# Attention maxima as two 64-row products side by side, in place of two 128-row products on block-diagonal keys

## The reference, cut to what matters

```python
scores = jnp.einsum('bhqd,bhkd->bhqk', query, key) / jnp.sqrt(D_K)
scores = jnp.where(m == 0, NEG_INF, scores)        # second layer only
probs = jax.nn.softmax(scores, axis=-1)
out = jnp.einsum('bhqk,bhkd->bhqd', probs, value)
...
x = x + jnp.tanh(g_xattn[1]) * (out @ Wo + bo)
```

## Time and profile before

| | |
|---|---|
| median of 3 runs | 2743.58 us (2742.97 to 2744.24) |
| the profiled execution | 2744.99 us |
| its span, first to last instruction | 2743.2 us |
| PE busy | 90% of the span, 12840 products |
| DVE, ACT, POOL busy | 53%, 39%, 18% |
| mean granted TensorE clock | 0.955 of full |
| attention, layer 0 / layer 1, one iteration in steady state | 52.82 us / 65.83 us |

### The profile page before, as it was taken

The page is one execution under the profiler, slowest core; times in us unless marked ns, Lnnn a source line. Parts: engine busy times, 40 slices in busy tenths (PEclk is TensorE's granted clock), DMA queues, the critical chain, the costliest instruction groups (busy, mean ns, idle before and its releaser), DMA issues. The chain is left out here.

```text
span 2743.2 us, 32089 instructions
## 1 busy us (share of the span) xinstructions
PE 2480.5 (90%) x12840; PEld 1860.6 (68%) x12864; DVE 1463.2 (53%) x2222; ACT 1078.3 (39%) x1734; POOL 505.4 (18%) x411
## 2 busy tenths in 40 slices
PE   4899999779999999996489999999579999999997
PEld 3557667458888888885355566665467788778776
DVE  4455565232222222211655665553488888888887
ACT  3233443243222222222223333332355666666564
POOL 1011211252000000001101111111462222222221
PEclk8799999889999999998699999999799999999999
DMA  3002111232001100102210111111321010101100
GB/s 129 31 16 81 59 47 47 86 114 81 16 31 46 46 27 20 47 31 75 95 41 28 59 59 59 59 44 62 100 82 53 16 46 32 47 16 34 44 16 31
DMA packets 87941, 140.92 MB, mean 51 GB/s; under 512 B 4848, under 2 KB 27760, under 8 KB 87792
## 3 DMA queue, kind: packets, MB, share of 16 engines
q1 hardware_dynamic: 87792, 138.87, 14.9%
HBM read 105.30 MB, written 33.55 MB: 51 GB/s over the span
## 5 line engine op out<-in xcount | busy, mean ns | idle before, releaser
L56 PE MATMUL l_ffn_hid<-l_ffn_xT_hi,l_ffn_w_hi 128*128 128x512 f32 x1024 | 406.0, 397 | 29.3 <-POOL l_ffn_w_lo L1124 29.3
L56 PE MATMUL l_ffn_acc<-l_ffn_w_hi,l_ffn_h_hi 128*128 128x512 f32 x1024 | 402.6, 393 | 18.1 <-DVE l_ffn_h_lo L1299 18.1
L56 PE MATMUL l_ffn_hid<-l_ffn_xT_hi,l_ffn_w_lo 128*128 128x512 f32 x1024 | 402.0, 393 | 0.0
L56 PE MATMUL l_ffn_hid<-l_ffn_xT_lo,l_ffn_w_hi 128*128 128x512 f32 x1024 | 401.9, 392 | 0.0
L56 PE MATMUL l_ffn_acc<-l_ffn_w_lo,l_ffn_h_hi 128*128 128x512 f32 x1024 | 399.5, 390 | 0.0
L56 PE MATMUL l_ffn_acc<-l_ffn_w_hi,l_ffn_h_lo 128*128 128x512 f32 x1024 | 399.2, 390 | 0.0
L1269 DVE TENSOR_TENSOR l_ffn_h_lo<-l_ffn_full,l_ffn_h_hi 128x512 fp32r<-128x512 f32 x128 | 88.6, 692 | 501.0 <-ACT l_ffn_h_hi L1181 501.0
L1136 POOL TENSOR_TENSOR l_ffn_at_next<-l_ffn_at_next,l_ffn_at_grid 128x512 f32<-128x512 f32 x128 | 187.5, 1465 | 491.7 <-ACT l_ffn_at_next L1197 491.6
L1176 ACT ACTIVATE l_ffn_full<-l_ffn_hid,l_ffn_b 128x512 f32<-128x512 f32 x128 | 88.2, 689 | 447.8 <-PE l_ffn_hid L56 447.8
L56 PEld LDWEIGHTS l_ffn_hid<-l_ffn_xT_hi,l_ffn_w_hi 128*128 128x128 f32 x1024 | 194.5, 190 | 76.0 <-POOL l_ffn_w_lo L1124 36.4
L56 PEld LDWEIGHTS l_ffn_acc<-l_ffn_w_hi,l_ffn_h_hi 128*128 128x128 f32 x1024 | 192.7, 188 | 65.0 <-DVE l_ffn_h_lo L1299 25.9
(11 more groups left out here) (191 smaller groups left out, 4309.3 us busy)
## 6 DMA issues: line engine op xcount, KB each, us to landing
stream<-l_att_xg SPq DMA_DIRECT2D x16, 1024.0 KB, 4.3
l_ffn_x_in<-stream SPq DMA_DIRECT2D x16, 1024.0 KB, 5.5
l_ffn_stage<-in_l_w SPq DMA_DIRECT2D x64, 256.0 KB, 2.8
l_ffn_xg<-stream SPq DMA_DIRECT2D x16, 1024.0 KB, 5.5
l_att_x_in<-in_x SPq DMA_DIRECT2D x8, 1024.0 KB, 6.5
l_att_xg<-in_x SPq DMA_DIRECT2D x8, 1024.0 KB, 5.3
stream<-l_ffn_xg SPq DMA_DIRECT2D x8, 1024.0 KB, 4.3
l_att_x_in<-stream SPq DMA_DIRECT2D x8, 1024.0 KB, 6.7
```

Source lines behind the costliest of these rows:

```text
L56: done = nc.tensor.matmul(out, lhs[a], rhs[b], start=first and n == 0, stop=last and n == len(passes) - 1)
```

## The change

In PE's `max_of` the product of half a takes only the 64 partitions on which its two heads lie, both of the weights and of the keys: partitions 0 to 63 for heads 0 and 1, 64 to 127 for heads 2 and 3. The zero rows of `keys.bd` outside a half are no longer multiplied; the result is the same. The two products are issued next to each other, on different rows of the array and to different banks. With the mask, both identity products come first, then both halves (before: identity, half, identity, half). Each half increments `max_ps`, so that DVE's waits count two per step. Number and size of the reductions, the weight loads (one ahead of each product) and the order around `max_of` stay.

```diff
@@ mask_front (DVE)
-                    dve.wait_ge(max_ps, NM * it)
+                    dve.wait_ge(max_ps, 2 * NM * it)
@@ max_of (DVE)
-                dve.wait_ge(max_ps, NM * it + m + 1)
+                dve.wait_ge(max_ps, 2 * (NM * it + m + 1))
@@ max_of (PE)
+                to = [score[:, 2 * (m % 2) + a, 0:2 * KEYS].rearrange("p (h k) -> p h k", h=2)
+                      for a in range(2)]
+                if masked:
+                    for a in range(2):
+                        nc.tensor.matmul(to[a], ident_bf[:, :], mask_add[:, q, :].unsqueeze(1)
+                                         .broadcast_to([P, 2, KEYS]), start=True, stop=False)
                 for a in range(2):
-                    to = score[:, 2 * (m % 2) + a, 0:2 * KEYS].rearrange("p (h k) -> p h k", h=2)
-                    if masked:
-                        nc.tensor.matmul(to, ident_bf[:, :], mask_add[:, q, :].unsqueeze(1)
-                                         .broadcast_to([P, 2, KEYS]), start=True, stop=False)
-                    done = nc.tensor.matmul(to, qT[it % QB][0][:, t, q * P:(q + 1) * P],
-                                            keys.bd[:, b, t, 2 * a:2 * a + 2, :],
-                                            start=not masked, stop=True)
-                done.then_inc(max_ps, 1)
+                    half = slice(2 * DH * a, 2 * DH * (a + 1))
+                    nc.tensor.matmul(to[a], qT[it % QB][0][half, t, q * P:(q + 1) * P],
+                                     keys.bd[half, b, t, 2 * a:2 * a + 2, :],
+                                     start=not masked, stop=True).then_inc(max_ps, 1)
```

## The result

The changed kernel takes 2786.75 us (median of 4 runs, 2784.08 to 2788.64), the kernel before, with a fourth run beside its first three, 2743.91: a ratio of 1.0156 with a 95% interval of 1.0143 to 1.0169, 43 us slower. The profiled execution of it is its fastest, 2784.08 us, with a span of 2782.3 us.

What follows compares the result with a forecast made beforehand. PE was taken to bound the steady iterations of both layers. The terms 18.5 + 19 - 2 + 4 gave +39.5 us on the profiled 2745.0, so 2784.5, or 2783 for the median; range 2766 to 2806.

Steps and rivals of the forecast that it cites:

- The overlap: In each step, the pair of 64-row halves streams together and costs one product, saving 0.14 us per step.
- The change of shape: On PE, each switch between 128-row and 64-row products costs 0.19 us, in either direction.
- layer 0: Steady iterations 1 to 6: 28 changes of shape less 16 savings, +3.1 us each, +18.5 us for six.
- Layer 1, steady: Iterations 1 to 6: 31 changes less the savings, 0.5 us absorbed by a wait; +3.15 us each, +19 us.
- DVE hides nothing: Steady layer 0: DVE needs about 0.93 us of a 1.22 us step, so it isn't the bound.
- The sign that I named: In the changed trace, DVE waits for PE at every reduction.
- The steps outside: Steps ahead of the loop and in iteration 0: -2 us in layer 0, +4 us in layer 1.
- Rival (a): No price for changing between 128 and 64 rows, only the saving is left: 2725 us; chance 0.07.
- rival (b): The pair of halves doesn't overlap, so 0.14 us per step isn't saved: 2808 us; chance 0.05.
- rival (c): The clock falls in the steady stretches too, +45 us: 2828 us; chance 0.06.
- rival (d): At changes of shape the gap exists but the weight load stays hidden, about +5 us: 2749 us; chance 0.03.

Runs made afterwards that it cites:

- e1: Changed kernel with half 1 first and on all 128 rows, half 0 on its 64, so nothing overlaps; 2830.46 us.
- e7: Changed kernel with two steps issued together, then two output products (layer 1: four identities, then four halves); 2764.37 us.
- e8: The grouping of e7 with 128-row products in place of 64-row halves, as its control; 2753.85 us.
- e3: Changed kernel with 64-row halves in layer 1 alone, layer 0 as in the kernel before; 2771.01 us.
- e4: As e3, but layer 1's steps of chunks 0 and 1 stay as in the kernel before; 2760.65 us.
- e5: Changed kernel's order and increments, but both products take all 128 rows; 2741.36 us, ratio 1.0001 to the kernel before.
- e6: Changed kernel with one increment of max_ps per step, on the second half, instead of two; 2785.59 us.
- e10: Changed kernel with 64-row halves only in layer 0's chunks 0 and 1 and the first two steps of later chunks, 128 rows elsewhere; 2737.32 us.
- e9: e3 with two more 64-row products of 512 columns behind each of layer 1's first 16 steps; 2771.02 us.

## Why the prediction was right

2783 was forecast and 2786.75 measured, inside 2766 to 2806, and the cause is the one that was named. That the number came so close is in part luck. In the profiled execution the stretches that the change touches came to +44.0 us where the sum had +39.5, and the untouched rest happened to be 4.9 us shorter.

- **The overlap** saves what the 32-row sets promised: 0.137 us per step by e1 and the changed kernel together, 0.14 forecast.
- **The change of shape** was taken as 0.19 from 32-row products, since no row had 64 rows. Measured is 0.196 in e1, where nothing overlaps. The changed kernel's layer 0 gives 0.198 (3.30 + 2.24 by 28) and e7 less e8 0.194 (0.48 + 2.24 by 14), both with 0.14 taken for the saving. As all 28 count, the small difference makes most of the 1.5 us by which layer 0 was undersized (20.0 for 18.5).
- **Layer 1, steady**: 18.9 for 19. The wait on DVE gave up 0.3 us (from 1.2 to 0.9) where I had counted on 0.5, and the order of the identities gave 0.2 back, which I had left in the bounds. The two misses offset each other.
- **DVE hides nothing** in the steady iterations: right, PE doesn't wait for it in layer 0. The sign that I named, DVE waiting at every reduction, was too strong: it waits at 10 of 16.
- **The steps outside** were the mis-sized term: +2 forecast, +5.1 in the trace. Layer 0's gain was 3.1, not 2, because these steps did not go at DVE's pace alone. The 16 ahead of the loop, and the later ones of iteration 0 with them, waited on PE too: the clock was 0.50 from 95 to 108 us, and DVE waited for PE at every second reduction,

```profile
96.41 1.51 DVE L667 TENSOR_REDUCE l_att_maxes<-l_att_score 128x4 f32<-128x616 f32 x2 [0.27 <-PE l_att_score L826]
```

a wait that is nearly gone in the changed kernel, at the same clock: 13.3 us from the first reduction to the last became 11.7. In layer 1 the pace at half clock was forecast well (0.35 slower; it is 1.18 against 0.81 to 0.83 at full clock before), but I took it for a third of the steps, and all of the first stretch and most of the second ran so. e3 less e4 puts it at 10 us. It stays within the ends of -6 to +9 about the value, as the whole did.
- Rival (a), no price between 128 and 64 rows, is refuted by the 0.33 and 0.34 in the timeline and by e1 and e5; rival (b) by the pair's common start; rival (c) by a mean clock of 1.00 in every steady iteration but the first of each layer, into which 3 and 1 us of half clock reach; rival (d) by the 0.34 between the first two output products.
- The packing rule of the page "TensorE: Matmul & The Clock Gate" of the Trainium skill (Part 3), by which (a) would have held, agrees with the trace inside the pair (0 to 6 ns from start to start) and has no term for its edges. The page "TensorEngine Tiling (Array Packing)" of the Trainium skill, under Key Properties, has a change of mode drain the engine. For 64 rows the trace agrees as far as it can show it: the pair's loads begin 0.33 behind the last 128-row product, 0.10 after the next product would have started.

What stays open: why the rest of the kernel, untouched, was 4.9 us shorter in the profiled execution. e6, alike there, was 3.3 us longer in it than the changed kernel, so it is about the scatter of runs (2784.08 to 2788.64); only a part is tied to the clock.

## What to carry to other kernels

Products that share the array, each on its own part of the rows, pay when many of the same shape follow one another; count the changes of shape per saved product before splitting one. Here a round trip of 0.4 us bought 0.14 for one pair, and 0.28 for two (e7) still lost. By these numbers it takes three pairs in a row to gain, an estimate that no run tests. Pairs among themselves gained (e10), so the same source line should have both forms. And where another engine sets the pace, time added on PE isn't safely hidden: changes of shape that fit under a reduction at full clock went with a stretch at half clock, where they don't fit.

## What was not expected

- The shape change has the same price within what the traces resolve, whatever stands on the other side: single (e1, 0.196 us) or paired (0.198), in layer 0 behind 512 columns, in layer 1 behind bfloat16 products of 308 (0.19, counting the wait and the order of the identities). These are averages over 28 or 31 changes, as many in as out.
- In layer 1's first 16 steps the whole stretch falls to half clock after the change, where the kernel before had a mean of about 0.9. A step grew from 0.82 us at full clock to 1.18, although by the prediction's count (0.73 us on PE) it would have stayed under the reduction's 0.80 at full clock. With an extra pair per step the clock returned after 6.8 us (e9). Less to stream is not the whole cause: in e1 the halves save nothing, and its stretch ran at half clock too (21.0 us); and in layer 0's first two chunks, where the steps stream less and change no shape, the time at half clock did not grow (58.6 us up to the end of iteration 0, 62.6 before). The gaps at the changes of shape are common to all five kernels whose clock fell in this stretch; no run has the gaps without 64-row products.
- Two bfloat16 identities in a row are 0.014 us per step cheaper than in turn with 32-bit products (e5, 65.60 for 65.82 us in the settled iterations).
